# A fused conv-gate and top-2 expert layer on one core: tile 0 of the experts taken from rows in SBUF, expert 0 placed first, and the line gates begun inside the transforms

## What is computed

```
x = x + conv_gate(layernorm_over_channels(x))
t = tokens(x)                                  # 2048 tokens of 256 channels
t = t + moe(layernorm(t))
```

```
S = sigmoid(xt @ Wg);  G, I = top_k(S, 2)
h = gelu(xt @ W1[e] + b1[e]);  y = h @ W2[e] + b2[e]      # 256 -> 1024 -> 256
out = sum over the two chosen experts of G * y
```

## Time and profile before

| | us |
|---|---|
| median of 3 runs | 382.37 |
| lowest and highest of them | 380.83 and 382.59 |
| the profiled execution, its own time | 382.42 |
| its span, first to last instruction | 380.2 |
| mean granted TensorE clock, share of full | 0.917 |
| busy: PE / PEld / DVE / ACT / POOL | 317.8 / 243.8 / 255.7 / 180.8 / 169.8 |

### The profile page before, as it was taken

The page is one execution under the profiler, slowest core; times in us unless marked ns, Lnnn a source line. Parts: engine busy times, 40 slices in busy tenths (PEclk is TensorE's granted clock), DMA queues, the critical chain, the costliest instruction groups (busy, mean ns, idle before and its releaser), DMA issues.

```text
span 380.2 us, 8711 instructions
## 1 busy us (share of the span) xinstructions
PE 317.8 (84%) x3114; PEld 243.8 (64%) x3114; DVE 255.7 (67%) x572; ACT 180.8 (48%) x486; POOL 169.8 (45%) x145
## 2 busy tenths in 40 slices
PE   1899995999913109899999999999999999999960
PEld 1677631457713109788888888887888888888830
DVE  3986599437799552678878877887887656555640
ACT  3355583615429632654564466456456433442420
POOL 7023292514009451036456655654565555444331
PEclk9989998999955555999999999999999999999995
DMA  7300000001222986346676666767775444344221
GB/s 245 103 1 3 0 0 3 0 28 55 71 69 93 299 193 211 121 91 159 157 182 178 155 172 181 171 137 171 184 167 108 77 87 62 72 80 73 32 31 22
DMA packets 36696, 40.32 MB, mean 106 GB/s; under 512 B 8400, under 2 KB 33232, under 8 KB 36656
## 3 DMA queue, kind: packets, MB, share of 16 engines
q1 hardware_dynamic: 29168, 29.56, 27.2%
q0 software_dynamic: 7488, 10.23, 15.7%
HBM read 30.20 MB, written 9.57 MB: 105 GB/s over the span
## 4 chain that ended last, share of the span: by engine, by line
PE 47%; DMA 28%; DVE 11%; issue 4%; POOL 3%; ACT 3%; POOLq 0%; SPq 0%; ACTq 0%; DVEq 0%
DMA out<-fb,idx 21%; PE ps L839 9%; PE ps L828 5%; PE ps L832 5%; PE ps L830 5%; PE ps L840 5%; PE ps L673 4%; DMA fb<-xn_rows,idx 4%; POOL wt L437 3%; PE ps L693 3%; PE ps L702 2%; DMA xt<-x_tok 2%; PE ps L706 2%; PE ps L709 2%; DMA xn_rows<-wt 2%
## 5 line engine op out<-in xcount | busy, mean ns | idle before, releaser
L628 ACT ACTIVATE fb<-ps,b1t 128x128 f32<-128x128 f32 x312 | 84.7, 384 | 104.8 <-issue 101.5
L828 PE MATMUL ps<-fb,wt 128*128 128x128 f16 x624 | 121.9, 221 | 1.6 <-DVE fb L1202 1.6
L830 PE MATMUL ps<-fb,wt 128*128 128x128 f16 x624 | 121.9, 221 | 0.0
L832 PE MATMUL ps<-fb,wt 128*128 128x128 f16 x624 | 121.9, 221 | 0.0
L496 POOL DMA_INDIRECT out<-fb,idx x39 | 74.4, 1908 | 101.6 <-DMA out<-fb,idx 56.0
L839 PE MATMUL ps<-wt,fb 128*128 x312 | 117.5, 379 | 1.4 <-DVE fb L1202 1.4
L840 PE MATMUL ps<-wt,fb 128*128 x312 | 85.0, 273 | 0.0
L828 PEld LDWEIGHTS ps<-fb,wt 128*128 x624 | 61.8, 99 | 32.3 <-issue 1.8
L830 PEld LDWEIGHTS ps<-fb,wt 128*128 x624 | 61.8, 99 | 3.0
L832 PEld LDWEIGHTS ps<-fb,wt 128*128 x624 | 61.8, 99 | 0.0
L486 POOL DMA_INDIRECT fb<-xn_rows,idx x39 | 43.8, 1122 | 26.2 <-issue 9.8
(11 more groups left out here) (186 smaller groups left out, 401.4 us busy)
## 6 DMA issues: line engine op xcount, KB each, us to landing
wt<-w SPq DMA_DIRECT2D x32, 512.0 KB
b2t<-b SPq DMA_DIRECT2D x39, 128.0 KB
xt<-x_tok SPq DMA_DIRECT2D x4, 512.0 KB, 7.7
out<-xt SPq DMA_DIRECT2D x8, 256.0 KB, 2.1
xn_rows<-wt SPq DMA_DIRECT2D x8, 256.0 KB, 2.1
b1t<-params SPq DMA_DIRECT2D x39, 4.0 KB
fb<-xn_rows,idx POOLq DMA_INDIRECT x39
out<-fb,idx POOLq DMA_INDIRECT x39, 4.7
```

Of the source, the lines that this page charges most:

```text
L628: a = nc.scalar.activation(hid[:, s, f * P:(f + 1) * P], h_ps(s)[:, f * P:(f + 1) * P], ACT.Gelu_apprx_tanh, bias=b1t[:, n % NBIAS, f:f + ...
L828: pe.matmul(dst, hi, xT[:, s, c * P:(c + 1) * P], start=(c == 0 and f % 4 == 0), stop=False, skip_group_check=True)
L830: pe.matmul(dst, hi, xT[:, s, (2 + c) * P:(3 + c) * P], start=False, stop=False, skip_group_check=True)
L832: m = pe.matmul(dst, lo, xT[:, s, c * P:(c + 1) * P], start=False, stop=(c == DC - 1), skip_group_check=True)
```

## The change

Two things are changed.

**Line gates.** The `w1d` matmul is cut into tiles 0 to 9, issued behind the DFT of image 5, and tiles 10 to 15 behind the last one (`gate_lines`); ACT takes the sigmoids of the first ten tiles behind image 5. DVE does the gates of tiles 0 to 5 between the last `power`s, the rest later; DVE_GATES is 13 now. `taps(1)` moves ahead of the small matmuls, the square root of `mag` ahead of the shifts, and the reduction `fm` is cut in two parts.

**Tile 0.** The counts are made such that expert 0 always has a tile and is placed first (`keybase`, `steps_of`), so its weights and biases are loaded by fixed addresses at the start, and are split inside the map loop (`split_hi` by ACT before u = 0 and at u = 2, 3, `split_lo` by DVE at b = 0..3). Tile 0's rows aren't gathered: a one-hot `first` picks them by 64 matmuls from `xrow` in SBUF, in transposed form. The token norm is done in three parts (`ROWS_AT`), the first two images' rows inside the map loop. `hot`, `pay` and `first` are built by one operation per block. The gate table comes after step 1. Place 1 may begin at tile 1 now, so its W1 quarters have to be split before step 1 and its W2 quarters before step 3 (`PLACE_FROM`, `QUARTERS_EARLY`).

```diff
-FIRST = SLOTS_MOST // P // E
+PLACE_FROM = [0] + [1 + -(-(SLOTS_MOST // P - 1) * p // (E - 1)) for p in range(E - 1)]
-LATE_ROWS = B - 2
+ROWS_AT = [0, 3, B - 1, B]
-DVE_GATES = 12
+EARLY_GATES = 10
+GATES_AT_ONCE = 3
+DVE_GATES = 13
...
         def quarters_at(n):
-            first = QUARTERS_FIRST if n == 0 else n + QUARTERS_AHEAD
-            return range(first, min(n + QUARTERS_AHEAD + 1, NQ))
+            ahead = [4, 7, 8] + list(range(10, NQ + 1))
+            return range(ahead[n], ahead[n + 1]) if n + 1 < len(ahead) else range(0)
...
+            for h in range(QUARTERS):
+                load(h)
+            biases(0)
-            for b in range(B):
+            for b in range(B - 1):
                 sp.wait_ge(t_done, b + 1)
...
-            for i in range(LEAD):
+            for i in range(1, LEAD):
                 gather(i)
...
+                if b == EARLY_GATES // 2:
+                    gate_sigmoids(0, slice(0, EARLY_GATES))
...
+            for h in range(DC):
+                split_hi(h)
...
             for u in range(B):
                 sigmoids(u)
                 if u in (0, 1, 4, 5):
                     shift(u + 4 if u < 2 else u + 2)
+                if DC <= u < QUARTERS:
+                    split_hi(u)
+                if u == B - 3:
+                    deviations(0)
+                if B - 3 <= u < B - 1:
+                    rows_hi(u - B + 3)
...
+                if b == EARLY_GATES // 2:
+                    gate_lines(slice(0, EARLY_GATES))
...
             taps(0)
+            pe.wait_ge(xlg_read, 1)
+            taps(1)
             pe.wait_ge(small_ready, 3)
             pe.matmul(ps[0:NT, 5, 128:256], dwm[:, :], wpwd[:, :], start=True, stop=False)
...
+            for k in range(NBLK):
+                if k % 4 == 0:
+                    pe.wait_ge(first_done, k // 4 + 1)
+                pe.wait_ge(xlo_done, k + 1)
+                for c in range(4):
+                    m = pe.matmul(ps[:, 0, c * P:(c + 1) * P], xrow[:, k, c * P:(c + 1) * P], first[:, k, :],
+                                  start=(k == 0 and c == 0), stop=(k == NBLK - 1), skip_group_check=True)
+            m.then_inc(xT_mm, 1)
...
+                for p in range(E):
+                    if n == PLACE_FROM[p]:
+                        pe.wait_ge(lo_done, QUARTERS_EARLY if p == 1 else QUARTERS * (p + 1))
+                if n == PLACE_FROM[1] + 2:
+                    pe.wait_ge(lo_done, 2 * QUARTERS)
...
+                if n == 0:
+                    pe.wait_ge(texp_done, 1)
+                    load_expert(1)
+                    turn(1)
             for n in range(TILES + 2):
+                if n == 2:
+                    table(2, 2, 6)
                 step(n)
...
             for b in (B - 2, B - 1):
+                gate_rows(GATES_AT_ONCE * (b - B + 2), GATES_AT_ONCE * (b - B + 3))
                 power(2 * b)
                 power(2 * b + 1)
...
+                if b < QUARTERS:
+                    split_lo(b)
                 if 2 <= b <= B:
                     add_x(b - 2)
                     stats_t(b - 2)
+                if b == B - 3:
+                    invert(0)
+            invert(1)
...
-            link(v.tensor_tensor(out=pay[:, 0], in0=by_tile, in1=over_tiles(place16[:, 1]), op=ALU.is_equal))
-            v.tensor_tensor(out=pay[:, 1], in0=pay[:, 0], in1=over_tiles(tok16[:, :, :]), op=ALU.mult)
             for a in range(TOP_K):
-                v.tensor_tensor(out=hot[:, a], in0=by_row, in1=place16[:, 0, a].unsqueeze(1).broadcast_to([P, P, NBLK]),
-                                op=ALU.is_equal).then_inc(hot_done, 1)
+                for k in range(NBLK):
+                    q = a * NBLK + k
+                    v.tensor_scalar(hot[:, q, :], iota16, minus_row[:, a, k:k + 1], 0.0, ALU.add, ALU.is_equal)
+                    ins = v.tensor_scalar(pay[:, q, 1, :], tiles16, tile_of[:, a, k:k + 1], cc("token")[:, k:k + 1],
+                                          ALU.is_equal, ALU.mult)
+                ins.then_inc(hot_done, 1)
+                if a == 0:
+                    invert(2)
...
+            over_tiles = lambda n: place16[:, n].rearrange("p a k -> p (a k)").unsqueeze(2).broadcast_to([P, 2 * NBLK, TCOL])
+            link(v.tensor_tensor(out=pay[:, :, 0, :], in0=tiles16.unsqueeze(1).broadcast_to([P, 2 * NBLK, TCOL]),
+                                 in1=over_tiles(1), op=ALU.is_equal))
+            for n in (2, 3):
+                ins = v.tensor_tensor(out=pay[:, :, n, :], in0=pay[:, :, 0, :], in1=over_tiles(n), op=ALU.mult)
+            ins.then_inc(hot_done, 1)
```

More of the change, by code:

```diff
@@ L678, in _ @@
             x_logits(B - 1)
[L680 to L682 removed]
+            gate_lines(slice(EARLY_GATES, NT))
             pe.wait_ge(tapw_done, 1)
@@ L716, in _ @@
                       par[0:1, PAR["bpwrow"]], start=False, stop=True).then_inc(small_mm, 1)
-            for u in range(1, 4):
+            for u in range(2, 4):
                 taps(u)
@@ L818, in step @@
                 for f in range(FC):
-                    for c in range(DC if one else 0):
+                    for c in range(DC if one and n > 0 else 0):
                         pe.lower_ap(piece(e1, c * F + f * P + P - 1, 1))
                         pe.lower_ap(piece(e1, PIECE + c * F + f * P + P - 1, 1))
-                    if two:
+                    if n > 2:
                         pe.lower_ap(piece(e2, 2 * PIECE + f * 2 * C, 2 * C))
@@ L963, in _, with gate, gate_stats, gate_rows @@
                 power(2 * (b - 2) + 1)
+            def gate(t):
+                dve.wait_ge(gate_row, t + 1)
+                gv = gated[:, t].rearrange("p (h w) -> p h w", w=W)
+                v.tensor_tensor(out=gv, in0=gv, in1=sg[:, t, H:H + W].unsqueeze(1).broadcast_to([P, H, W]),
+                                op=ALU.mult).then_inc(gated_done, 1)
+            def gate_stats(t):
+                if t < DVE_GATES:
+                    dve.wait_ge(gated_done, t + 1)
+                else:
+                    dve.wait_ge(gate_col, t - DVE_GATES + 1)
+                return v.bn_stats(gbn6[:, t, :], gated[:, t, :])
+            def gate_rows(first, end):
+                for t in range(first, end):
+                    if t < DVE_GATES:
+                        gate(t)
+                    if t > 0:
+                        gate_stats(t - 1)
             for b in (B - 2, B - 1):
+                gate_rows(GATES_AT_ONCE * (b - B + 2), GATES_AT_ONCE * (b - B + 3))
                 power(2 * b)
@@ L1185, in _ @@
-            ins.then_inc(hot_done, 1)
+            slots = psum_pick[:, 0]
+            link(v.tensor_tensor(out=lowest[:, :], in0=slots[:, 0], in1=slots[:, 1], op=ALU.min))
+            iota16, tiles16 = c16[:, C16["iota"]], c16[:, C16["tiles"]]
+            v.tensor_scalar(near[:, :, :], slots, -(P - 1) / 2, MULTIPLES, ALU.add, ALU.add).then_inc(dve_step, 1)
+            steps[0] += 1
+            for k in range(NBLK):
+                ins = v.tensor_scalar(first[:, k, :], iota16, lowest[:, k:k + 1], None, ALU.is_equal)
+                if k % 4 == 3:
+                    ins.then_inc(first_done, 1)
@@ new lines, in _ @@
+            dve.wait_ge(dve_step, steps[0])
+            v.tensor_scalar(tile_of[:, :, :], near[:, :, :], MULTIPLES, 1.0 / P, ALU.subtract, ALU.mult)
+            link(v.scalar_tensor_tensor(out=minus_row[:, :, :], in0=near[:, :, :], scalar=MULTIPLES, in1=slots,
+                                        op0=ALU.subtract, op1=ALU.subtract))
+            for a in range(TOP_K):
+                for k in range(NBLK):
+                    q = a * NBLK + k
[5 more added lines that the diff above has]
+                    invert(2)
```

294 lines of the change are left out of this document (143 added, 151 removed).

## The result

The changed kernel takes 383.26 us in the median (381.15 to 385.76, 20 runs), the kernel before 380.02 on the same chip (377.77 to 382.60, 20 runs). The ratio of the two is 1.0082, 95% interval 1.0061 to 1.0103: 3.1 us slower. I had said 381.1 against 382.4, no measurable change. The profiled execution of the changed kernel took 384.88 us, its span is 382.7 (before 380.2).

What follows compares the result with a forecast made beforehand. The PE was taken to bound steps 2 to 38, so only step 2's start counted: +2.1 us, with −3.35 at the front, gave −1.25, from 382.4 to 381.1 us. Range 376.5 to 386; middle case 0.37.

Steps and rivals of the forecast that it cites:

- Step 1 released by the copy, not a DMA: Start of step 1: DVE's copy of tile 1, ending at 152.65, releases it, since gather 1 lands at 147.9.
- Step 2 at 156.62, forecast 156.8: Start of step 2: 160.1 on the old clock, near 156.8 with the earlier map loop start, at full clock.
- the front: Line gates up to the map loop's start: −1.6 us, or −3.35 us if the clock does not fall.
- `hot`/`pay` pairs: One-hot building on DVE: 0.165 for an operation, 0.21 with a second pointer, so pairs spaced by 0.375 us.
- From the logits to the index: Routing and one-hots: logits begin at 109.6, index at 139.75, 14.15 us later than the old 125.60.
- From the index to step 1: DVE's path from the index at 139.75 through splits and payloads to the copy of tile 1, ending at 152.65.
- the slower rival: Clock stays at half through the gate table and into step 2: 385.2 us, 387 with the front's fall; chance 0.27.
- The payloads: Three DVE payload operations before tile 1's copy: upper bound of 1.49 us each taken, 4.3 in all; lower bound 0.78.
- 55 to 45: Clock in `taps(5)` before the map loop: 55 in 100 that it does not fall, worth 1.75 us.
- The step that failed: Steps 2 to 38 keep their matmuls' pace, so the whole effect shows in step 2's start, 158.03 before.
- −1.25: Whole kernel: step 2's start +2.1 us, with the front's −3.35, gives this change in time, called not measurable.
- my rivals: Faster, short operations and payloads cheap: 374.6, chance 0.36; slower, half clock: 385.2, 0.27; step 1 waits for a gather: near 383.

Runs made afterwards that it cites:

- e2_copy: Changed kernel with the t_out wait once and VectorE's copy of tile 1's transposed rows moved ahead of choosing the gates and the payloads: ratio 0.9943 to the kernel before.
- e4_best: Changed kernel with t_out wait once, tile 1's copy early, last rows as before and lines(0, 4) behind the bias term: 376.07 us against 380.59 for the kernel before.
- e3_gates_only: Kernel before with only the line-gate part of the change, nothing of tile 0, scatter-adds' waits as before: ratio 0.9974 to the kernel before.

## Why the prediction was wrong

- **Held.** Step 1 released by the copy, not a DMA: yes, at 151.09. Step 2 at 156.62, forecast 156.8. The way there is off in parts that cancel: the map loop started 3.8 us later than forecast, and from there to step 2 it took 3.9 us less. That step 2 came within 0.2 us is luck. `sigmoids(6)` 4.27 us later with a table load on each side of `rows_hi(0)`, forecast 3.8 plus the front's shift; logits 4.15 later, of which 3.7 from ScalarE as worked out; `hot`/`pay` pairs spaced by 0.36 in the first half and 0.42 in the second (0.375 forecast), `first` by 0.163 (0.165). From the logits to the index it took 28.2 us, forecast 30.15: the table's 16 matmuls took 0.71 and not 1.9, with `hot` and `pay` contiguous now. From the index to step 1 it took 12.9, as forecast. Step 1 took 4.4 us and not 5.0, the gate table 1.31 and not 2.4; the clock came back within step 1, so the slower rival's mechanism didn't happen here; its state came only in e2_copy and e4_best, behind a rest that their order makes.
- **The payloads** cost 1.49 and 1.45 us each, the upper bound that I took against the 0.78 of the old ones (4.41 for the three, where the sum had 4.3):

```profile
146.18 1.49 DVE L1270 TENSOR_TENSOR wt<-c,place 128x1280 f16<-128x1280 f16 x1
147.70 2.89 DVE L1273 TENSOR_TENSOR wt<-wt,place 128x1280 f16<-128x1280 f16 x2
```

  They took 1.16 ns per element, as the 1.19 of L872. The Trainium skill's "Vector Engine (DVE) Microarchitecture Reference", section 5.1, reports that a two-source operation with 2-byte operands, one of them read at an innermost step of 0, ran one element per cycle; the trace agrees. L953, of which I had written that it fits this, doesn't bear on it: it has one source and took 0.64 ns per element.
- **The front, mis-sized.** "−3.35 us for the map loop's start" measured +0.44 in the profiled run. The aggregates end at 59.8 (60.0 forecast), and the last small matmul came 0.64 us earlier and not 1.6. I had left out that the early sums start GpSimd's `rf`, which was idle there before: the chain's operations took 1.3 us more, and the clock fell, on which I had set 55 to 45 that it doesn't. With GpSimd kept out the map loop starts at 63.4 to 65.7 in five traces, 2.8 to 5.1 us earlier than before, so the forecast's size is there. The median gains of the gates, 3.3 us with tile 0 and 1 alone, are less sure than that.
- **The step that failed:** "Steps 2 to 38 follow at the pace of their matmuls and the change leaves their work as it is, so whatever the change is worth must show in one moment, the start of step 2". The mechanism was wrong here, not only a size. The earlier trace rows showed a PE busy 41.97 of 42 us, and I took the pace of the PE for that of the kernel. A second chain ran beside it, the scatter-adds, 39 of them one behind the other, which carried 21% of the path before. It was behind in both kernels while weights were loaded; with 0.5 us more in each link it no longer caught up afterwards. The 3.9 us lost after step 2 are 0.5 up to the rows of tile 0, 1.1 from there to those of tile 38 (206.5 us and not 205.4) and 2.4 behind them. TensorE stayed busy in 158 to 200 us in the changed kernel too (42.00 us), so this share could not have warned; GpSimd's waits for its own DMA, 26 of 39 adds, could. And I had read the line `t_out` as a wait that is met by then, so as nothing. With that one line undone the kernel measured 0.9965, −1.3 us, where I had forecast −1.25; that too is partly luck, since the parts of the sum up to step 2 were off and cancelled.

None of my rivals had this mechanism. The range held the median, the sign was missed.

## What to carry to other kernels

When a profile shows one engine fully busy, look for a second chain that needs nearly as long per round, here an indirect DMA that waits for the one before it, and count every instruction of its link, waits that are met too. Put the wait that will be late first in the list, and take waits that hold once for all out of the loop. And before work is started early on an idle engine, see which short operations of another engine on the path will run beside it. And an earlier start behind a rest of TensorE can be a start at half clock, as in e2_copy: price the work behind it at both levels.

## What the runs showed of the hardware

- An indirect DMA on GpSimd's queue starts 0.27 us after its late semaphore if that wait is the first of those ahead of it, and 0.74 to 0.86 if another wait, already met, stands ahead of it. All eighteen traces fit: where the wait for the add before stands first (13 kernels) the median gap behind it is 0.27 (up to 0.79 where the rows, whose wait comes second, were done shortly before), where it stands second (five kernels) it is 0.78 or 0.79.
- An indirect DMA that GpSimd started inside VectorE's two-source operation of 1.22 us ended 1.45 to 1.47 us after that operation did, in each of twelve in a row in the changed kernel (293 to 354 us). Where it started in the operation's first 0.4 us it took 2.3 to 2.6 us, instead of 1.59.
- Small VectorE operations on SBUF beside a GpSimd one: 0.47 to 0.54 us instead of 0.17 to 0.23, in the same places in the changed kernel and in e3_gates_only; the copy out of PSUM between them took 0.16 in both cases.
- The gate table's 32 matmuls of 80 columns, at a granted clock of 0.50 both times, took 4.82 us with `hot` and `pay` strided and 2.31 with both contiguous (e2_copy).
